# A decoder layer on one core: dense tiles apart in the sorted stage, rounds reordered, ScalarE normalises the rows, second products lag in the last stage

## The reference

```python
x = _layernorm(x + attn(x))     # 16 heads of 16, causal softmax
x = _layernorm(x + by_token(x)) # expert of a token = its id // 3125, E = 4, F = 256
x = _layernorm(x + moe(x))      # expert of a token = argmax(x @ Wr + br), E = 4, F = 1024

# by_token, for expert e of the token; all three weights are ctx_2048[e]
g = silu(einsum('bsd,fd->bsf', x, C[e])); u = einsum('bsd,fd->bsf', x, C[e])
y = einsum('bsf,df->bsd', g * u, C[e])

# moe: softmax(x @ Wr + br), its largest entry top_w and that expert's
y = (silu(x @ Wg[e]) * (x @ Wu[e])) @ Wd[e] * top_w
```

## Time and profile before

| | |
|---|---|
| median of 3 runs | 320.68 us |
| profiled execution | 321.15 us, span 319.3 us |
| busy: TensorE, VectorE, ScalarE, GpSimd | 256.0, 192.4, 134.1, 68.5 us |
| chain that ended last, by engine | PE 55%, DVE 18%, issue 9%, ACT 6%, POOL 6%, DMA 5% |
| granted TensorE clock, mean | 0.929 |

### The profile page before, as it was taken

One profiled execution on the slowest core, in us unless ns is written; L12 is line 12 of the kernel. 1 busy time (PEld: TensorE's weight loads), 2 busy tenths in 40 slices (PEclk: granted clock), 3 DMA queues, 4 the chain that ended last, 5 costly groups with the idle time before them and its releaser, 6 DMA issues.

```text
span 319.3 us, 5964 instructions
## 1 busy us (share of the span) xinstructions
PE 256.0 (80%) x2039; PEld 169.4 (53%) x2040; DVE 192.4 (60%) x415; ACT 134.1 (42%) x223; POOL 68.5 (21%) x127
## 2 busy tenths in 40 slices
PE   4785689889988775869678547976999999999990
PEld 4364456556755543546466432443666656666570
DVE  3868687775986374787636653575554445445441
ACT  3461565856938541754233240563332313333220
POOL 8400000000232352041101375000222211222222
PEclk9799799999999989699899657899999999999997
DMA  6999072420333445487000012420000000000000
GB/s 194 350 303 279 4 262 69 135 66 3 118 117 93 141 108 175 110 300 283 0 0 2 4 56 74 118 67 0 18 16 3 0 13 16 16 16 16 9 9 7
DMA packets 17416, 28.51 MB, mean 89 GB/s; under 512 B 2733, under 2 KB 12974, under 8 KB 17392
## 3 DMA queue, kind: packets, MB, share of 16 engines
q1 hardware_dynamic: 16048, 25.28, 25.8%
q0 software_dynamic: 1344, 2.90, 2.5%
HBM read 19.43 MB, written 9.50 MB: 91 GB/s over the span
## 4 chain that ended last, share of the span: by engine, by line
PE 55%; DVE 18%; issue 9%; ACT 6%; POOL 6%; DMA 5%; SPq 1%; POOLq 0%; DVEq 0%; ACTq 0%
PE ps L1255 33%; PE ps L1625 3%; DVE arena L941 3%; PE ps L1365 3%; PE ps L1326 2%; ACT wf_hi L540 2%; POOL sorted L502 2%; PE ps L1564 2%; DMA ring<-wqkvT 2%; PE ps L1261 2%; PE ps L1322 1%; DMA sorted<-X,pos_i 1%; DVE wf_lo L775 1%; DVE arena L936 1%; DVE arena L915 1%
## 5 line engine op out<-in xcount | busy, mean ns | idle before, releaser
L1255 PE MATMUL ps<-wf_hi,arena 128*128 x336 | 82.2, 329 | 6.3 <-DVE wf_lo L775 3.1
L1255 PE MATMUL ps<-wf_lo,arena 128*128 x168 | 55.2, 328 | 0.0
L1255 PEld LDWEIGHTS ps<-wf_hi,arena 128*128 128x128 f16 x336 | 32.8, 98 | 30.7 <-issue 10.9
L719 ACT ACTIVATE arena<-ps 128x512 f32<-128x512 f32 x22 | 13.1, 597 | 62.3 <-PE ps L1255 62.3
L775 DVE SCALAR_TENSOR_TENSOR wf_lo<-ring,wf_hi 128x1024 f16<-128x1024 f32 x17 | 20.6, 1219 | 11.2 <-ACT wf_hi L540 6.0
L1174 DVE SCALAR_TENSOR_TENSOR arena<-ps,arena 128x512 f32<-128x512 f32 x22 | 15.2, 692 | 17.9 <-PE ps L1625 9.6
L1255 PE MATMUL ps<-xT_hi,arena 128*128 (+1 forms) x88 | 22.7, 321 | 1.8 <-DVE arena L1113 1.1
L1255 PEld LDWEIGHTS ps<-wf_lo,arena 128*128 128x128 f16 x168 | 16.4, 98 | 9.2
L941 DVE TENSOR_REDUCE arena<-ps 128x4 f16<-128x1024 f32 x16 | 19.6, 1223 | 1.2 <-PE ps L1326 1.2
L517 POOL TENSOR_SCALAR veps<-mv 128x1 f32<-128x1 f32 x11 | 2.5, 225 | 82.5 <-DVE mv L1194 82.5
L1255 PE MATMUL ps<-arena,xT_hi 128*128 128x512 f16 (+1 forms) x64 | 16.5, 348 | 3.7 <-DVE arena L896 2.8
(11 more groups left out here) (225 smaller groups left out, 532.8 us busy)
## 6 DMA issues: line engine op xcount, KB each, us to landing
ring<-Wf SPq DMA_DIRECT2D x17, 512.0 KB, 3.8
sorted<-fill SPq DMA_DIRECT2D x1, 4515.0 KB, 21.0
arena<-Wf SPq DMA_DIRECT2D x7, 512.0 KB, 6.9
arena<-sorted SPq DMA_DIRECT2D x20, 129.0 KB, 2.2
sorted<-fill SPq DMA_DIRECT2D x1, 1161.0 KB, 6.5
ring<-xT SPq DMA_DIRECT2D x4, 256.0 KB, 5.5
X<-x_tok SPq DMA_DIRECT2D x1, 1024.0 KB, 7.9
ring<-ctxT SPq DMA_DIRECT2D x2, 512.0 KB, 3.6
```

Source lines behind the costliest of these rows:

```text
L719: a.activation(sg[:, half * 512:(half + 1) * 512], ps[:, 2 * half, :], ACT.Silu, scale=1 / W_SCALE).then_inc(sg3, 1)
L1255: last = t.matmul(dst, xs(k), ws(k), start=(k == 0 and m == 0), stop=(k == nk - 1 and m == 2))
```

## The change

- **Sorted stage.** The dense tiles stand at places 3 and 6 (`DENSE_AT`). Their two hidden halves are transposed through banks 2 and 7, one behind the other. The transpose x2T moves from tile s-4 at the end of TensorE's round to tile s-5 behind the first transpose, with ScalarE's copy likewise. VectorE no longer normalises the rows: it makes `shift` = -mean * rstd (128 x 1) for tile s-4 behind `res` of tile s-3, and ScalarE writes the row with an Identity activation (scale rstd, bias shift) at the end of its round. `res`, `shift`, statistics and aggregate stand at the end of VectorE's round.
- **Splits.** Attention splits 11 chunks: none in steps 12, 14 and 15, two in step 13. The four of the sorted stage go to the rounds one and three behind each dense tile. Behind the window of three the last stage has 8: two ahead of tile 0, two in each of tiles 0, 1 and 2.
- **Tables.** One dummy Silu behind the last `OT_hi` and one behind the last router Exp.
- **TensorE in attention.** Expert numbers are loaded in the head between the first score groups. `out_project(2)` goes ahead of `values` of its step. The four keep-warm matmuls ahead of the last projection go, and four of the ten behind the last scatter.
- **GpSimd.** Two scatters instead of one stand among the last reciprocal roots.
- **Last stage.** TensorE does tiles 0, 1 and 2, then down(0), tile 3 with down(1) ahead of its second half, down(2), and from tile 4 on the old order. Hidden halves of tiles 0 and 1 have buffers of their own (`h_of`). VectorE does statistics and finish of tile 0 behind tile 2, those of 1 and 2 behind tile 3.

```diff
-B_AT = NA
+DENSE_AT = (3, 6)
-        ATT_LO = (0, 1, 1, 1, 1, 0, 1, 1, 1, 0, 1, 1, 1, 0, 1, 1)
+        ATT_LO = (0, 1, 1, 1, 1, 0, 1, 1, 1, 0, 1, 1, 0, 2, 0, 0)
-        BETWEEN = (1, 2, 3, 4)
+        BETWEEN = 2 * TB
+        ENDING = ((2,), (1, 1), (1, 1), (1, 1))
...
# GpSimd
-            for i in range(NS - 1):
+            for i in range(NS - 2):
                 inv_std2(i)
             scatter3(0, 0)
+            inv_std2(NS - 2)
+            scatter3(0, 1)
             inv_std2(NS - 1)
...
# ScalarE, end of attention; then its rounds
+            a.activation(sg_s[:, 0:1], identF[:, 0:1], ACT.Silu)
...
+                i = s - 5
+                if 0 <= i < NS:
+                    act.wait_ge(x2T_rdy, i + 1)
+                    if i >= 1:
+                        act.wait_ge(lg_rdy, i)
+                    a.activation(x2T, ps[:, 5, 0:D].rearrange("p (k t) -> p k t", k=NK),
+                                 ACT.Copy).then_inc(x2T_sb, 1)
...
                 i = s - 4
                 if 0 <= i < NS:
-                    act.wait_ge(x2T_rdy, i + 1)
...
+                    act.wait_ge(sh2, i + 1)
+                    a.activation(XS[:, i, 0:D], res[i % 2], ACT.Identity, bias=shift[:, i % 2:i % 2 + 1],
+                                 scale=rstd[:, i % 2:i % 2 + 1]).then_inc(x2_rdy, 1)
...
             exps_router(len(PARTS) - 1)
+            a.activation(sg[:, 0:1], identF[:, 0:1], ACT.Silu)
...
# VectorE's rounds
-                i = s - 4
-                if 0 <= i < NS:
-                    dve.wait_ge(rs2, i + 1)
-                    v.tensor_scalar(XS[:, i, 0:D], res[i % 2], mv[:, i % 2, 0:1], rstd[:, i % 2:i % 2 + 1],
-                                    ALU.subtract, ALU.mult).then_inc(x2_rdy, 1)
...
                 if 0 <= j < NS:
+                    dve.wait_ge(y2, j + 1)
+                    if j >= 2:
+                        dve.wait_ge(x2_rdy, j - 1)
+                    v.scalar_tensor_tensor(out=res[j % 2], in0=ps[:, (3, 4)[j % 2], 0:D], scalar=inv,
+                                           in1=XS[:, j, 0:D], op0=ALU.mult, op1=ALU.add).then_inc(r2, 1)
+                i = s - 4
+                if 0 <= i < NS:
+                    dve.wait_ge(rs2, i + 1)
+                    v.scalar_tensor_tensor(out=shift[:, i % 2:i % 2 + 1], in0=mv[:, i % 2, 0:1], scalar=-1.0,
+                                           in1=rstd[:, i % 2:i % 2 + 1], op0=ALU.mult,
+                                           op1=ALU.mult).then_inc(sh2, 1)
...
# VectorE's last stage
+            for i in range(PEEL):
+                splits = ENDING[i + 1] if i + 1 < len(ENDING) else (0, 0)
+                tile(i, i % 2, first=i == 0, splits=[range(n, n + splits[0]), range(n + splits[0], n + sum(splits))])
+                n += sum(splits)
+                if i == 2:
+                    ending(0, 0)
+            ending(1, 1)
+            ending(2, 0, 1)
...
# TensorE, attention
+                if b == B - 1 and g == project_at(b):
+                    out_project(b - 1)
                 if step >= 1:
                     values(step - 1)
...
-            keep_warm(4, wf_hi[:, 0:512], bank=0)
...
# TensorE, last stage
+                if behind is not None:
+                    down(*behind)
                 gate_up(p, 1, expert)
-                if not first:
-                    down(i - 1, expert_of(i - 1) if before is None else before)
...
-            keep_warm(WARM_GAP + 2, wf_hi[:, 0:512])
+            keep_warm(WARM_GAP // 2 + 2, wf_hi[:, 0:512])
...
+            first = [tile(0, 0, first=True), tile(1, 1), tile(2, 0)]
+            down(0, first[0])
+            tile(3, 1, behind=(1, first[1]))
+            down(2, first[2])
```

More of the change, by code:

```diff
@@ L620, in _ @@
                     exps(b, g)
+                if b == B - 1 and g == 1:
+                    for _ in range(ATT_LO[step]):
+                        split_hi(n)
+                        n += 1
                 if b >= 1 and g == 1:
@@ L627, in _ @@
                     q_odds(stacked_at(step))
-                for _ in range(ATT_LO[step]):
-                    split_hi(n)
-                    n += 1
+                if not (b == B - 1 and g == 1):
+                    for _ in range(ATT_LO[step]):
+                        split_hi(n)
+                        n += 1
                 if projected_at(step) is not None:
@@ L672, in _ @@
                     if k >= 1:
-                        act.wait_ge(y2, i if k != B_AT else B_AT)
+                        act.wait_ge(y2, max(p for p in range(i) if p not in DENSE_AT) + 1)
                     a.activation(hs_hi, ps[:, 2, 0:D].rearrange("p (k t) -> p k t", k=NK),
@@ L1042, in _ @@
                     stacks(stacked_at(step))
-                for _ in range(ATT_LO[step]):
+                for _ in range(min(1, ATT_LO[step])):
                     split_lo(n)
@@ L1047, in _ @@
                     o_lo(b - 1)
+                for _ in range(ATT_LO[step] - 1):
+                    split_lo(n)
+                    n += 1
                 if projected_at(step) is not None:
@@ L1200, in finish, with tile @@
                                 ALU.subtract, ALU.mult).then_inc(f3, 1)
-            def tile(i, p, first=False, last=False, scattered=None, splits=()):
+            def tile(i, p, first=False, last=False, splits=((), ())):
                 gated(i, 0)
@@ L1634, in down, with tile @@
                     pe.wait_ge(c_lo, NCH)
-                three(ps[:, 7, 0:D], lambda k: h_hi[:, k], lambda k: h_lo[:, k],
+                hi, lo = h_of(i)
+                three(ps[:, 7, 0:D], lambda k: hi[:, k], lambda k: lo[:, k],
                       lambda k: wf_hi[:, bass.ds(expert * EW + DOWN + k * D, D)],
                       lambda k: wf_lo[:, bass.ds(expert * EW + DOWN + k * D, D)], NF).then_inc(y3, 1)
-            def tile(i, p, before=None, first=False, last=False):
+            def tile(i, p, first=False, last=False, behind=None):
                 expert = expert_of(i)
```

208 lines of the change are left out of this document (103 added, 105 removed).

## The result

The changed kernel is slower, by 1 to 2%: 327.14 us (median of four runs, 325.52 to 329.45) against 320.88 us for the kernel before beside it, a ratio of 1.016 with a 95% interval of 1.010 to 1.022. In a second series beside other runs of the kernel before it was 327.33 against 320.96, 1.0215 (1.0145 to 1.0286). Medians are of all executions; the ratios leave out those more than 1.5% above the fastest of their kernel, so they aren't quite the quotients of the medians. The prediction was 316.4 with a range up to 321.3, so its sign is wrong.

A forecast was written before the change was run, and what follows sets the result against it. TensorE bounds the last stage, waits between engines the sorted stage, GpSimd's issues the second scatter's stage. Against the profiled 321.15 us, -4.7 - 2.9 - 1.0 + 4.3 = -4.3 gives 316.9, 316.4 against the median; range 311.5 to 321.3.

The forecast's parts named there:

- End of attention: Up to a_lo(0): the later of two paths, sorted-stage rows and last batch, comes 3.5 to 5.5 us earlier, taken 4.7.
- Head: Expert loads between the first four score groups: TensorE's idle time covers nearly all, 0 lost, at most 1 us.
- Early tables, dense tiles apart: Sorted stage: table and splits take 2.1 us off rounds 0 to 3; separate banks give 35.8 for rounds 4 to 10, now 36.9.
- rival 5: Identity switches the activation table: two loads of 1.28 us in each round would make it 345; chance 2%.
- The ordinary round: Sorted-stage round without a dense tile: 3.45 us against 3.27 undisturbed now, so ordinary rounds gain nothing from ScalarE.
- what would be wrong: Signs against the forecast: rounds above 4 us, over four table loads, first stage not 3 shorter, no stall before down(2).
- Rival 3: Slower: ScalarE's normalisation closes each round's chain, TensorE's part doubles at half clock; 320.9 to 324.4; 18% with a cancelling sum.
- Between the stages: Between sorted and last stage: six keep-warm matmuls instead of ten, partly offset by the third split; 1.0 us less, bounds 0 and 1.6.
- Last stage: Lagging second products: +1.8 us at tile(2), 0.0 to -0.2 at down(0), +2.8 at down(2); sum +4.3, bounds 2.5 and 6.
- Rival 2: With fewer keep-warm matmuls TensorE may enter the sorted and last stages at half clock: 2.5 us more, 318.9; chance 13%.
- Nothing is late next: Last stage behind down(2): no further cost, since from tile 4 the order is the old one.

The follow-up runs named there:

- e3: Changed kernel with the last stage's second products in the old order, one pair of h buffers, eight weight pieces split ahead of the first second product: 321.8 us.
- e5: Changed kernel with two buffers for the high and low parts of the sorted rows' products instead of one: 323.4 us, ratio 1.0035 to the kernel before.
- e1: Changed kernel with VectorE instead of ScalarE normalising the rows of the sorted stage: 319.8 us, ratio 0.9931 to the kernel before.
- e7: Changed kernel with each sorted-stage round's second transpose, and its copy, behind the first product instead of ahead of it: 316.3 us, ratio 0.9846 to the kernel before.
- e4: Changed kernel with unread products filling the last stage's two long stalls, ten ahead of down(0), eight ahead of down(2): 324.8 us, ratio 1.0104 to the kernel before.

## Why the prediction was wrong, point by point

- **End of attention** (predicted 4.7 earlier): 4.4. GpSimd's add at 0.22, the residual at 110.33 (predicted 109.8), the second scatter's landing 2.7 instead of 4.4. Right, with what the head cost inside it.
- **Head** (0, at most 1): 2.25 lost, about 1.3 regained later. The step that failed is that TensorE's idle time between the groups would cover nearly all: I counted one 0.64 us wait for two loads, seen where TensorE had other work. Behind the first score group, with three loads, TensorE stood for 2.47 us, and VectorE then waited for it.
- **Early tables, dense tiles apart.** Rounds 0 to 3 took 7.9 us (120.5 to 128.4), where 7.6 were predicted, and the first dense tile's rounds 4 to 6 took 15.2 (to 143.6) for 15.3. Right. The table stays loaded through the stage: four loads in the trace, so rival 5 is out.
- **Where the 5.9 us of the sorted stage lie.** Rounds 7 to 9 took 18.6 us (to 162.2) instead of 16.1; of these 2.5, 1.5 are the second dense product at a lower clock (4.12 for 2.62). From there to the last logits it took 23.1 instead of 19.9, 3.2 more: these are the rounds without a dense tile and the drain.
- **The ordinary round, 3.45 us: this failed, in two terms.** It takes 3.99 at the full clock; e3, with the same sorted stage, has two such rounds in a row, 3.99 and 4.00, where the changed kernel's second took 5.53, at 0.69 of the clock. The first term: the Identity was priced by copies, at 0.38 to 0.41; it takes 0.60. The trace of before had no activation with two operands read per partition, and I gave the missing row no upper bound. The Trainium skill (ScalarE: Activation LUTs, What ACT_TABLE_LOAD costs) gives a price: 186 ns and 0.833 ns per element with immediate operands, and about 93 ns for each pointer operand of 128x1. An estimate from this page for 256 elements with both operands is 585 ns; the trace shows 600. With copies from SBUF at 407 ns here (its 399), the page and the trace agree. The second term: the walk had `hs_lo` in the chain, but not the copy to `hs_hi` ahead of it, 0.38 us, which waits for `y2` of the tile before; with two buffers (e5) the round is 3.38. The "what would be wrong" list named rounds above 4 us; this one is at 3.99.
- **What that did.** The prediction had the stage 2.9 less than before; it came out 3.0 more, by 3.7 us of added idle time. With VectorE normalising (e1) it is 57.5, 3.4 less than before. That is the price of giving the row to ScalarE, shift and handover with it: 4.2 us of waits, 6.4 in this profile. The Identity's wrong price is only some 0.2 of the 0.38 in a round, about 2.2 us in eleven by my estimate; no run isolates it. The wrong conclusion was that ScalarE's normalisation leaves the ordinary rounds as they are.
- **Rival 3** described the closed chain, 0.5 us a round more. It had 18% and named 320.9 to 324.4; measured are 327.1, since the last stage was missed too. It looked for the price in the half clock; against the kernel before, the runs show it in idle time, and TensorE's busy time is 0.7 less. Against it I wrote that half-clock stretches were in the rows that I priced; the waits of the new chain were not.
- **Between the stages** (1.0 less): 1.3 less, though TensorE idles 0.9 for VectorE's third split.
- **Last stage** (+4.3): +7.2. The stalls are what was predicted to 0.1 us (1.60, 1.82, 3.08, 2.73), the last ended by VectorE's statistics; e7, where only one clock drop is left, has 113.0 with 1.6 of clock in it, so 4.4 of stalls. The missing term is the clock, put at nothing and worth 2.4 to 3.0. Rival 2 looked for it at the stage's first tile and not behind the stalls that the same text had just added. "Nothing is late next" was wrong in that sense only.
- **Sum.** -4.4 + 3.0 - 1.3 + 7.2 = +4.5, the span's 4.4.

What stays open: why the clock of the sorted stage differs between kernels. The runs give the waits (4.2 us of TensorE's idle time for the engine, 0.9 for the buffer, 3.8 for the place of the transpose). The rest, 2.2, 2.7 and 4.7, is faster work, and one profile each can't tell how much of it belongs to the edit, when unchanged code varies by 3.2.

## What to carry to other kernels

Before moving an operation to another engine, find a row with the same kinds of operands; if there is none, take a bound from above and ask whether the operation stands in a chain that closes in each round. In such a loop the place of a transpose in TensorE's queue was worth as much waiting as the choice of engine, 3.8 and 4.2 us. Price each stall that an edit adds for its length, and set as a bound beside it the slow products that may follow, here 1.35 to 1.6 us for 36; where a buffer's write waits for a read one round back, write that wait into the walk. And compare TensorE's busy and idle time over a stage before reading a gain as a shorter wait.

## What the runs showed of the hardware that was not expected

- An activation on 128x256 from SBUF takes 407 ns as Copy and 600 ns with bias and scale read per partition.
- Three value loads in a row left TensorE idle for 2.47 us behind the first score group, 0.82 each; in the seven profiles with the loads there it was 1.46 to 2.49.
- A stall of TensorE of about 3 us was followed by slow products in some executions and not in others: 6.80 us for the 36 in the changed kernel, 5.44 in e7 and 5.45 in the kernel before, behind the same 3.08. Behind 4.22 us (e3) they took 7.05, behind filled stalls 5.55 (e4). The Trainium skill (TensorE: Matmul & The Clock Gate, Part 1) has the throttled clock as the default and activity as what lifts it; the filled stalls agree.
